# Attention with whole-array maxima from the scores' own stacks, and text sums added up on GpSimd first

## What is computed

```python
q = rms_norm(x @ w_q.T + b_q, g_q)          # 16 heads of 32
k, v         = rms_norm(ctx_txt @ w_k.T + b_k, g_k), ctx_txt @ w_v.T + b_v
k_img, v_img = rms_norm(ctx_img @ w_k_img.T + b_k_img, g_k_img), ctx_img @ w_v_img.T + b_v_img
def attention(q, k, v, kv_mask=None):
    s = jnp.einsum('bqhd,bkhd->bhqk', q, k) * SCALE
    if kv_mask is not None: s = jnp.where(kv_mask[:, None, None, :], s, -1e9)
    return jnp.einsum('bhqk,bkhd->bqhd', softmax(s), v)
out = (attention(q, k, v, kv_mask) + attention(q, k_img, v_img)) @ w_o.T + b_o
```

## Time and profile before

| | us |
|---|---|
| median of 3 runs (lowest, highest) | 3864.08 (3860.53, 3866.32) |
| the profiled execution, its own time | 3863.82 |
| its span, first to last instruction | 3861.6 |
| attention stage, from its first to its last work | 864 to 2900 |

### The profile page before, as it was taken

One profiled execution on the slowest core, in us unless ns is written; L12 is line 12 of the kernel. 1 busy time (PEld: TensorE's weight loads), 2 busy tenths in 40 slices (PEclk: granted clock), 3 DMA queues, 4 the chain that ended last, 5 costly groups with the idle time before them and its releaser, 6 DMA issues. The chain is left out here.

```text
span 3861.6 us, 55479 instructions
## 1 busy us (share of the span) xinstructions
PE 3348.9 (87%) x18048; PEld 1824.0 (47%) x18048; DVE 2314.6 (60%) x3780; ACT 1534.5 (40%) x2933; POOL 15.7 (0%) x34
## 2 busy tenths in 40 slices
PE   6999999967999999999999999999985651799993
PEld 5877777753333333333333333333324430677772
DVE  5766666646466666666666666666635658433335
ACT  3444334322455555555555555555551110122222
POOL 0000000000000000000000000000000000000000
PEclk8999999987899999999999999999997775899997
DMA  5666666685435253443525344452404542101004
GB/s 147 164 166 168 164 166 167 167 119 122 103 69 112 61 115 72 100 93 80 110 63 115 72 101 91 82 111 62 104 6 136 163 153 86 69 22 44 22 22 174
DMA packets 405977, 402.04 MB, mean 104 GB/s; under 512 B 43568, under 2 KB 326256, under 8 KB 403320
## 3 DMA queue, kind: packets, MB, share of 16 engines
q1 hardware_dynamic: 363272, 367.44, 40.4%
q10 hardware_dynamic: 42624, 33.56, 2.6%
HBM read 262.98 MB, written 137.92 MB: 104 GB/s over the span
## 5 line engine op out<-in xcount | busy, mean ns | idle before, releaser
L834 ACT ACTIVATE at_probs<-at_st 128x512 f32<-128x512 f32 (+1 forms) x1664 | 913.8, 595 | 940.0 <-PE at_st L713 932.4
L862 DVE TENSOR_REDUCE at_cm<-at_mx 128x2 f32<-128x896 f32 x768 | 822.2, 1090 | 555.9 <-PE at_mx L729 555.9
L713 PE MATMUL at_st<-at_qst,at_kst 101*128 101x512 f32 (+1 forms) x1664 | 705.1, 470 | 73.9 <-ACT at_probs L834 50.7
L713 PEld LDWEIGHTS at_st<-at_qst,at_kst 101*128 101x128 f32 (+1 forms) x1664 | 271.3, 184 | 679.5 <-issue 344.1
L764 PE MATMUL at_acc<-at_probs,at_ones 128*32 128x512 f32 (+2 forms) x3584 | 471.7, 601 | 22.0 <-ACT at_ev L814 22.0
L752 PE MATMUL at_acc<-at_probs,at_vt 128*32 128x512 f32 (+2 forms) x3584 | 478.7, 608 | 0.9 <-ACT at_probs L834 0.9
L729 PE MATMUL at_mx<-at_kmx,at_qmx 33*128 33x448 f32 (+1 forms) x2048 | 386.0, 429 | 43.3 <-DMA at_kmx<-stack_rows 33.4
L729 PEld LDWEIGHTS at_mx<-at_kmx,at_qmx 33*128 33x128 f32 x2048 | 185.7, 188 | 263.6 <-issue 230.0
L862 DVE TENSOR_REDUCE at_top<-at_mx 128x2 f32<-128x514 f32 x256 | 176.9, 691 | 137.5 <-PE at_mx L729 137.5
L1274 ACT ACTIVATE ff_h<-ff_psa,ff_b1c,alpha 128x512 f32<-128x512 f32 x128 | 99.6, 779 | 378.3 <-PE ff_psa L1256 378.3
L764 PEld LDWEIGHTS at_acc<-at_probs,at_ones 128*32 128x32 f32 (+2 forms) x3584 | 107.0, 110 | 300.1 <-issue 237.0
(11 more groups left out here) (182 smaller groups left out, 4030.6 us busy)
## 6 DMA issues: line engine op xcount, KB each, us to landing
at_kst<-k_high SPq DMA_DIRECT2D x256, 200.1 KB
at_kmx<-k_high SPq DMA_DIRECT2D x64, 400.2 KB
at_kst<-k_low SPq DMA_DIRECT2D x128, 200.1 KB
pj_xin<-in_ctx_dram SPq DMA_DIRECT2D x96, 256.0 KB, 4.2
k_high<-pj_kh SPq DMA_DIRECT2D x96, 256.0 KB, 3.1
k_low<-pj_kl SPq DMA_DIRECT2D x96, 256.0 KB, 4.7
values<-pj_vs SPq DMA_DIRECT2D x96, 256.0 KB, 4.5
at_vt<-values SPq DMA_DIRECT2D x32, 768.0 KB
```

The source lines that it names most:

```text
L713: pe.matmul(st[0:kn, h % 2, :], kst[p][:, h, t * P:t * P + kn], qst[p][:, h, :], start=True, stop=True).then_inc(S["st_done"], 1)
L834: act.activation(probs[0:kn, SLOT[t], h, :], st[0:kn, h % 2, :], ACT.Exp, scale=SCALE).then_inc(S["exp_done"], 1)
L862: dve.tensor_reduce(dst, mx[:, 2 * slot:2 * slot + 2, 0:kn], AX.X, ALU.max).then_inc(S["mx_free"], 1)
```

## The change

Seven things change together, all in `attend`.

1. Maxima no longer have stacks of their own. They read the first 97 rows of the scores' stacks (`MROWS`), one matmul per head over the whole array, 64 in a group. The stacks `at_kmx`, `at_qmx` and their loads are gone; the scores' stacks and the values have three buffers, not two, and are loaded two groups ahead.
2. The maxima's places are by single matmul: one behind each of heads 0, 1 and 2, three behind head 3.
3. POOL adds the probabilities of text tiles 0, 1, 2, 3, 4, 7, 8 and 9 into `at_added` (seven additions of 128x2048). PE then needs 7 sum passes, not 14: tiles 5, 6, the two halves of 10, `at_added`, 11 and 12, placed at steps 6, 7, 11 and 12 and in steps 0 and 1 of the next group.
4. POOL forms V_txt*S_img + V_img*S_txt and S_txt*S_img; DVE does one reciprocal, not two, and two more operations.
5. The ring of probabilities has five slots, not four.
6. `ev` and `res` have one buffer, not two.
7. The loop runs over three groups at a time; SP's queue is written out without a loop.

```diff
+    MROWS = ROWS + 1
...
+    SUMMED = [(5, 0, P), (6, 0, P), (10, 0, HALF), (None, 0, P), (11, 0, P), (10, HALF, P), (12, 0, KLAST)]
+    NSUM, SUM_IMG0 = len(SUMMED), 4
+    SUMS_AT = {(6, 0): [0], (7, 0): [1], (11, 0): [2], (12, 1): [3]}
+    SUMS_LATE = {(0, 1): [4], (1, 1): [5, 6]}
+    TEXT = [0, 1, 2, 3, 4, 7, 8, 9]
+    NADD = len(TEXT) - 1
+    JOIN_AT = 4
+    RING = 5
+    SLOT = [0, 1, 2, 3, 4, 0, 1, 2, 0, 1, 2, 3, 4]
+    TRIPLES = GROUPS // 3
...
-        kst = [a.sb(f"kst{p}", [STACK, HG, SK], F32R) for p in range(2)]
-        qst = [a.sb(f"qst{p}", [STACK, HG, SQ], F32R) for p in range(2)]
-        kmx = [a.sb(f"kmx{p}", [HALF + HD + 1, 2, SK + 1], F32R) for p in range(2)]
-        qmx = [a.sb(f"qmx{p}", [HALF + HD + 1, 2, SQ], F32R) for p in range(2)]
-        vt = [a.sb(f"vt{p}", [P, KT, P]) for p in range(2)]
+        kst = [a.sb(f"kst{p}", [STACK, HG, SK + 1], F32R) for p in range(3)]
+        qst = [a.sb(f"qst{p}", [STACK, HG, SQ], F32R) for p in range(3)]
+        vt = [a.sb(f"vt{p}", [P, KT, P]) for p in range(3)]
         probs = a.sb("probs", [P, RING, HG, SQ])
+        added = a.sb("added", [P, HG, SQ])
...
+        places = [(t, h) for t in range(KT) for h in (0, 1, 2, 3, 3, 3)]
+        for n in range(2 * NPAIR):
+            plan.setdefault(places[n], []).append((n // 2, n % 2))
+        top_at = {(11, 1): 0, (11, 3): 1}
...
-            load_max(0, 0, 0)
-            load_stack(0, 0, 0)
-            load_max(1, 1, 0)
-            load_values(0, 0)
...
+            load_stack(0)
+            load_values(0)
+            load_stack(1)
+            for G in range(GROUPS):
+                if G + 2 < GROUPS:
+                    if G:
                         sp.wait_ge(S["st_done"], NST * G)
-                    load_stack(G + 1, 1 - par, nxt)
-                if not (isinstance(G, int) and G + 2 >= GROUPS):
-                    sp.wait_ge(S["mx_full"], NPAIR * (G + 1))
-                    load_max(G + 2, par, i + 1)
-                if not last:
-                    if not known(G, 1):
-                        sp.wait_ge(S["v_done"], NPASS * G)
-                    load_values(G + 1, 1 - par)
-                if not known(G, 1):
-                    save(G - 1, i if par else i - 1, 1 - par)
-
-            pairs(sp, body)
-            save(GROUPS - 1, GROUPS // 2 - 1, 1)
-            for p in range(2):
-                sp.wait_ge(saved[p], 16 * (GROUPS // 2))
+                    load_stack(G + 2)
+                if G + 1 < GROUPS:
+                    if G >= 2:
+                        sp.wait_ge(S["v_done"], NPASS * (G - 1))
+                    load_values(G + 1)
+                if G:
+                    save(G - 1)
...
+            sets = [(kst[p][0:MROWS, :, SK:SK + 1], 0.0) for p in range(3)]
+            sets += [(qst[p][ROWS:MROWS, :, :], 1.0) for p in range(3)]
...
+            def join(g):
+                pool.wait_ge(S["v_free"], 2 * g.G + 2)
+                pool.wait_ge(S["s_free"], 2 * g.G + 2)
+                if not g.first:
+                    pool.wait_ge(S["res_done"], g.G)
+                pool.tensor_tensor(part[:, 0, :], ev[:, VT, :], ev[:, SI, :], ALU.mult).then_inc(S["joined"], 1)
+                pool.tensor_tensor(part[:, 1, :], ev[:, VI, :], ev[:, ST, :], ALU.mult).then_inc(S["joined"], 1)
+                pool.tensor_tensor(rl[:, 0, :], ev[:, ST, :], ev[:, SI, :], ALU.mult).then_inc(S["joined"], 1)
+                pool.wait_ge(S["joined"], 4 * g.G + 2)
+                pool.tensor_tensor(rl[:, 1, :], part[:, 0, :], part[:, 1, :], ALU.add).then_inc(S["joined"], 1)
+
+            def add(g, n):
+                t = TEXT[n + 1]
+                pool.wait_ge(S["exp_done"], NST * g.G + HG * (t + 1))
+                if n:
+                    pool.wait_ge(S["add_done"], NADD * g.G + n)
+                elif not g.first:
+                    pool.wait_ge(S["s_done"], NSUM * g.at(-1).G + SUM_IMG0)
+                so_far = added[:] if n else probs[:, SLOT[TEXT[0]]]
+                pool.tensor_tensor(added[:], so_far, probs[:, SLOT[t]], ALU.add).then_inc(S["add_done"], 1)
+
+            def body(g):
+                for n in range(NADD):
+                    if n == JOIN_AT and not g.first:
+                        join(g.at(-1))
+                    add(g, n)
...
-                for r in range(2):
-                    at = slice(r * HALF, r * HALF + HD + 1)
-                    done = pe.matmul(mx[:, 2 * slot + r, 0:kn], qmx[p][at, j, qt * P:(qt + 1) * P],
-                                     kmx[p][at, j, k0:k0 + kn], start=True, stop=True)
-                done.then_inc(S["mx_full"], 1)
+                pe.matmul(mx[:, bank, 0:kn], qst[w.j][0:MROWS, h, qt * P:(qt + 1) * P], kst[w.j][0:MROWS, h, k0:k0 + kn],
+                          start=True, stop=True).then_inc(S["mx_full"], 1)
...
+                if t is None:
+                    pe.wait_ge(S["add_done"], NADD * (g.G + 1))
                 for h in range(HG):
                     cols = slice(h * HD, (h + 1) * HD)
-                    done = pe.matmul(acc[cols, 1, :], ones[r0:r1, :], probs[r0:r1, SLOT[t], h, :],
-                                     start=q in (0, IMG0), stop=q in (IMG0 - 1, NPASS - 1))
+                    src = added[:, h, :] if t is None else probs[r0:r1, SLOT[t], h, :]
+                    done = pe.matmul(acc[cols, 1, :], ones[r0:r1, :], src,
+                                     start=q in (0, SUM_IMG0), stop=q in (SUM_IMG0 - 1, NSUM - 1))
...
+                w = None if g.last else g.at(1)
+                before = None if g.first else g.at(-1)
                 for t in range(KT):
-                    for run in range(2):
-                        for h in (2 * run, 2 * run + 1):
-                            scores(G, i, par, t, h)
-                        if not last:
-                            for m in plan.get((t, run), []):
-                                maxima(G + 1, Wi, 1 - par, m)
-                            if (t, run) in top_at:
-                                tops(G + 1, top_at[t, run])
-                        if t == 0 and not known(G, 1):
-                            for q in (12, 13):
-                                if run == 0:
-                                    values(G - 1, *before, q)
-                                else:
-                                    sums(G - 1, q)
-                        elif t > 0 and run == 0:
-                            values(G, i, par, t - 1)
-                            sums(G, t - 1)
+                    for h in range(HG):
+                        scores(g, t, h)
+                        if w:
+                            for m, r in plan.get((t, h), []):
+                                maxima(w, m, r)
+                            if (t, h) in top_at:
+                                tops(w, top_at[t, h])
+                        if h == 1:
+                            if t > 0:
+                                values(g, t - 1)
+                            elif before:
+                                for q in (12, 13):
+                                    values(before, q)
+                        if h % 2:
+                            if before:
+                                for q in SUMS_LATE.get((t, h // 2), []):
+                                    sums(before, q)
+                            for q in SUMS_AT.get((t, h // 2), []):
+                                sums(g, q)
...
-                    dve.reciprocal(rl[:, k, :], ev[p][:, s, :]).then_inc(S["fin"], 1)
-                    dve.tensor_tensor(part[:, k, :], ev[p][:, v, :], rl[:, k, :], ALU.mult).then_inc(S["fin"], 1)
+                dve.wait_ge(S["joined"], 4 * g.G + 4)
+                dve.reciprocal(part[:, 1, :], rl[:, 0, :]).then_inc(S["fin"], 1)
+                dve.scalar_tensor_tensor(part[:, 0, :], rl[:, 0, :], bv[:, bass.ds(g.G, 1)], rl[:, 1, :], ALU.mult, ALU.add).then_inc(S["fin"], 1)
+                dve.wait_ge(S["fin"], 2 * g.G + 2)
+                if not g.first:
+                    dve.wait_ge(S["saved"], 16 * g.G)
+                dve.tensor_tensor(res[:], part[:, 0, :], part[:, 1, :], ALU.mult).then_inc(S["res_done"], 1)
```

More of the change, by code:

```diff
@@ L555, in _, with __init__, at, below @@
             tokens(nc, dve, step)
+class Group:
+    def __init__(self, i, j):
+        self.i, self.j = i, j
+        self.G = 3 * i + j
+        self.known = isinstance(i, int)
+        self.first = self.known and self.G == 0
+        self.last = self.known and self.G == GROUPS - 1
+    def at(self, step):
+        j = self.j + step
+        return Group(self.i + (j // 3), j % 3)
+    def below(self, n):
+        return self.known and self.G < n
 def attend(nc, scratch, out_t, b_v, b_v_img):
@@ L808, in copy_top @@
                                ACT.Copy).then_inc(S["top_copied"], 1)
-            def evacuate(G, p, kind, bank, done, free):
-                act.wait_ge(S[done], NPASS * G + (IMG0 if kind < VI else NPASS))
-                if kind == VT and not known(G, 2):
```

(31 more changed lines are left out.)

242 lines of the change are left out of this document (108 added, 134 removed).

## The result

The changed kernel takes 3849.55 us (median of 5 runs, 3846.39 to 3851.55) beside 3865.11 us before (5 runs, 3860.53 to 3869.16): ratio 0.9959 [0.9945, 0.9974]. That is 15.6 us faster, where 128 were forecast. Its profiled span is 3846.9 us. The changed kernel itself ran only here and beside e5 to e8 (3848.95), so differences to it in e1 to e4 and e9 to e12 are across series.

The account below looks back on a forecast made before the run. PE's order was taken to set the pace, with DVE late next. 44.3 + 13.2 = 57.5 us a group, taken as 57.0, plus 0.4 gave 57.4; 31 x (61.48 - 57.4) = 126 off 3863.8: 3738, stated as 3736, range 3650 to 3825.

Parts of the forecast that it names:

- rival (4): PE's clock falls once in each group: 57.4 + 6.2 = 63.6 us a group, 3930 us in all; chance 0.06.
- Prices on PE: PE's matmul of 512 columns 0.23 us, array form change 0.20, pass 0.86; step without a sum pass 3.20 us.
- Maxima about even: Maxima on PE: three pairs with their changes 1.14 us a step before, six whole-array matmuls 1.08 after.
- The DVE loop: Third maxima pair directly ahead of next step's first, so PE waits for DVE's reduction: 4.15 us a step, 0.83 still.
- Rival (1): DVE paces the group as forecast: 56 to 58.5 us a group, 3694 to 3772 us; chance 0.58.
- both parts of the sum: A group's steps 0 to 9 at 44.3 us and steps 10 to 12 at 13.2, together 57.5, taken as 57.0.
- Wait at the turning: At a group's end PE waits about 0.6 us for the negation, two scores behind the last maxima.
- POOL's price: POOL's addition takes 4.4 us for 128x2048 (bounds 1.8 and 6.0) and 1.2 for 128x512.
- POOL beside DVE: POOL's last addition may hold the negation's last, two-operand operation on DVE: 0.4 us a group, at worst 4.4.
- Start and end: Attention stage starts 5 us later and saves about 5 us at its end; the two cancel.
- POOL's ones: At the start POOL first writes three rows of 2048 ones: 5.3 us, before 3.8.

Follow-up runs that it names:

- e5: Changed kernel with the later turning of e1 and the maxima in whole pairs behind heads 1, 2 and 3: 3613.75 us, ratio 0.9351.
- e8: Changed kernel with three needless matmuls of 448 columns ahead of the turning: 3789.14 us, ratio 0.9808.
- e1: Changed kernel with each half of the turning (of the negated maxima) two heads later: 3714.88 us, ratio 0.9546.
- e4: Changed kernel with all 14 sum passes on PE, POOL adding no tiles and only joining: 3984.18 us, ratio 1.0233.
- e9: Kernel of e5 with POOL's last addition in a group waiting for the negation's TENSOR_SCALAR: 3614.0 us.
- e12: Kernel of e5 run once more, unchanged: 3611.8 us, ratio 0.9337.
- e10: Changed kernel with one wait added on POOL, so the seventh addition starts after the negation: 3720.75 us, ratio 0.9612.
- e3: Changed kernel with POOL adding seven tiles, not eight; tile 9 goes back to PE as a sum pass: 3760.63 us, ratio 0.9664.
- e6: Changed kernel with the later turning of e1 and maxima places (0, 1, 2, 2, 3, 3): 3642.0 us, ratio 0.9424.
- e11: Kernel of e5 with the turning back at the changed kernel's early place: 3800.96 us, ratio 0.9821.
- e2: Changed kernel with six needless matmuls of 448 columns ahead of the turning: 3770.69 us, ratio 0.9686.

## Why the prediction was wrong

The failed step is the clock, a term that the sum put at nothing. The sum took a middle group at the full clock, and rival (4), a fall in each group, stood at 0.06, with the argument that a wait of 0.45 us in a middle group had left the clock high. That wait says nothing of one of 1.49 us, and the prediction itself put a wait of 0.6 plus a hold of unknown length ahead of the same instruction. It added the two as time and never as a gap. The balance of a group, forecast 57.4 to measured 61.44: clock 3.1 (e10; 3.3 in e8), hold 1.1 instead of 0.4, the rest +0.2. Without the fall 31 x 3.1 = 96 us more would have been gained.

- **Prices on PE.** Three maxima in a row span 0.77 us, 0.20 apart: as forecast. The whole of a plain step was too low: 3.20 forecast, 3.3 to 3.9 in e5. A sum pass is worth 0.9 (e3) to 1.06 (e4), where 0.86 was forecast.
- **Maxima about even:** right as work (e4). The Trainium skill's rule (TensorEngine Tiling (Array Packing), Theoretical Speedup) of up to twice the throughput, from which I estimated 6.4 us a group for doing without two row tiles, doesn't show: PE's busy time fell by 0.4.
- **The DVE loop:** right, with its cause. Step 10 begins 43.8 us after step 0 in the changed kernel (44.3 forecast), and taking the third pair's place away (e5) removes the waits. But PE stands still about 0.58 us six times a group (57.1 us in 99 waits, 16.3 groups), not 0.83 in ten, since its own work is longer than I had. Rival (1), with POOL out of the way, is e10: groups of 57.20, 3720.75 us, beside 57.4 and 3736. Steps 0 to 9 take 43.8 us there and steps 10 to 12 13.4, beside 44.3 and 13.2: both parts of the sum came out.
- **Wait at the turning:** 0.6 forecast, 0.4 without the hold.
- **POOL's price:** 4.57 us for an addition (4.4), 1.28 to 1.30 for 128x512 (1.2). The Trainium skill's 4497 ns (GPSIMD Engine Reference, Elementwise — side-by-side cycle accounting) is nearer than my extrapolation from the earlier trace rows.
- **POOL beside DVE:** the hold is real and mis-sized, 1.1 us instead of 0.4, and it hits another instruction: not the last operation with two inputs, but the TENSOR_SCALAR ahead of it, with one. The Trainium skill (SBUF — State Buffer, Who interferes with whom) has both cases, and names tensor_scalar among those that can take the shared ports; the traces agree, up to 3.1 us in e5. An operation with two inputs is held too (e9, section 8: 0.65 to 1.78 us), though not the one that the prediction named. By its size alone the hold would have given 58.1 a group and some 3757 us, within the range.
- **Start and end:** -4.6 at the end (-5). At the start +10.5 instead of +5. POOL's ones took 5.51 us (5.3 forecast). The loads come to 4.7, as forecast: the first maximum starts 2.4 us later in the stage (877.06 beside 877.74, less the two starts 861.10 and 864.20), and head 1's k lands 2.3 us after PE wants it (880.08). What was missing is that the first group's maxima run alone at clock 0.50, as before, but now one by one: PE's busy time in this stretch went from 22.96 to 31.45 us.
- **Rival (4)** had the right mechanism and double the price: 6.2 us were read from group 1, where the fall was longer (0.90 on average over 67.7 us is some 13.5 us at 1.2 GHz, not 10.2) and PE hardly waited for anything; a fall costs 3.1 to 3.4 here. With its real price "it decides from a fall in two groups of three on" becomes "it eats three quarters of the gain".

## What to carry to other kernels

Sum up the waits that will meet ahead of one PE instruction, and treat the total as a gap in PE's work that can cost the clock besides its own length. An instruction that waits for a short chain on another engine belongs behind work that is there anyway: here one line in a table was worth 4.8 us a group (135 us in all), and a second one 2.8 more (101 us). When an engine that was idle gets work, look at what short instructions of its neighbour fall beside that work, because they can wait for its end; and check the gain of a filled wait by the next wait behind it, as in e9.

## What the runs showed of the hardware

- A DVE TENSOR_SCALAR of 128x32 (fp32 in, bf16 out, both in SBUF) takes 0.19 us alone and lasts to the end of a running POOL addition: 1.27 us (after), 2.40 (e6), 3.11 (e5). The TENSOR_REDUCE ahead of it (L908) took 0.20 us beside the same addition.
- A DVE SCALAR_TENSOR_TENSOR of 128x512 with two inputs from SBUF is held by a running POOL addition as well: 0.65 us (after), 1.78 (e9). A RECIPROCAL of 128x512 is not: 3.35 us in both.
- Where PE stood still 1.49 us at the turning (3.0 in e11) the clock went to 1.2 GHz for some 10.2 us in each middle group, in the wait or just behind it, although PE was busy 56 of 61.4 us in the group and had work nearly without a gap for those 10 us. Where it stood still 0.3 to 0.6 us (e2, e3, e10, e5) the clock stayed up in the middle groups; at 0.82 to 0.92 (e8) it fell in two runs of four groups and once more for 6.8 us, and not in the others. What decides among these last was not found.
- Needless work can be worth its time: six matmuls more in each group made the kernel 79 us faster.
